# Two-layer graph network, one core: the one-hots' numbers and the directions are read from PSUM instead of SBUF

## What is computed

```python
# layer 0
h   = x @ W_lin.T
ef  = shifted_softplus(gaussian(edge_weight) @ Wf1 + bf1) @ Wf2 + bf2      # (edges, 128)
agg = segment_sum(h[src] * ef, dst)
x   = layernorm(x + shifted_softplus(agg @ Wm1 + bm1) @ Wm2 + bm2)
# layer 1: 32 scalars and 32 vectors of 3 per node
w  = silu(silu(emb(edge_weight) @ w0 + b0) @ w1 + b1) @ w2 + b2            # 4 x 32 per edge
Y1 = sqrt(3) * edge_attr / |edge_attr|                                      # directions (edges, 3)
ss, vv = (x[:, :32] @ W_up0)[src], (x[:, 32:] @ W_up1)[src]
m0, m3 = w[0] * ss, w[3] * (vv . Y1)
m1, m2 = w[1] * ss * Y1, w[2] * vv
x = layernorm(x + segment_sum([m0, m3, m1, m2], dst) @ W_out)
```

## Time and profile before

| | us |
|---|---|
| median of 3 runs (2197.67 to 2209.35) | 2200.56 |
| profiled execution, its own time | 2202.79 |
| span of the profiled execution | 2201.0 |
| busy: PE / DVE / ACT / POOL | 1899.1 / 1370.4 / 637.9 / 1569.6 |
| granted clock of PE, mean | 0.823 |

### The profile page before, as it was taken

How to read it: one execution, slowest core, us unless ns; L and a number is a source line. 1 busy time by engine, 2 the same in 40 slices (tenths; PEclk the granted TensorE clock), 3 DMA queues, 4 the chain that set the end, 5 groups by cost and what they waited for, 6 DMA issues and landing times.

```text
span 2201.0 us, 34359 instructions
## 1 busy us (share of the span) xinstructions
PE 1899.1 (86%) x10138; PEld 1431.4 (65%) x10138; DVE 1370.4 (62%) x2905; ACT 637.9 (29%) x995; POOL 1569.6 (71%) x1599
## 2 busy tenths in 40 slices
PE   5887877778777887777879999999999999899997
PEld 4665666666666666666557777666776676677766
DVE  6755555555555555555645776666667666666665
ACT  3643343343433433432541111111111111111114
POOL 4777777777777777777147777777777777777770
PEclk8777777777777777777867998898999998988889
DMA  7422222222222222222021111111121221111112
GB/s 217 126 78 78 76 81 76 76 81 76 76 81 76 80 76 76 81 76 62 6 82 51 55 54 53 53 54 54 53 55 54 54 55 54 52 55 54 53 52 66
DMA packets 105683, 152.31 MB, mean 69 GB/s; under 512 B 33982, under 2 KB 65490, under 8 KB 105546
## 3 DMA queue, kind: packets, MB, share of 16 engines
q0 software_dynamic: 50656, 103.11, 17.3%
q1 hardware_dynamic: 54652, 46.76, 7.0%
q10 hardware_dynamic: 336, 2.01, 0.3%
HBM read 138.53 MB, written 13.21 MB: 69 GB/s over the span
## 4 chain that ended last, share of the span: by engine, by line
POOL 68%; issue 22%; PE 7%; DMA 1%; DVE 1%; ACT 1%; SPq 0%; POOLq 0%; DVEq 0%; ACTq 0%
POOL sent L436 68%; DMA unit_in<-in_x 1%; PE bank L984 1%; PE bank L800 1%; PE bank L767 1%; PE bank L815 1%; PE bank L953 1%; PE bank L759 1%; PE bank L988 0%; PE bank L942 0%; PE bank L871 0%; PE bank L879 0%; PE bank L802 0%; DMA sent<-up_table,senders 0%; DMA sent<-h_table,senders 0%
## 5 line engine op out<-in xcount | busy, mean ns | idle before, releaser
L436 POOL DMA_INDIRECT sent<-up_table,senders x784 | 775.3, 989 | 268.2 <-issue 237.7
L436 POOL DMA_INDIRECT sent<-h_table,senders x784 | 766.5, 978 | 263.9 <-issue 238.6
L815 PE MATMUL bank<-onehot,msg 128*128 128x128 f32 x4704 | 794.0, 332 | 7.1 <-DVE sums L1098 4.2
L815 PEld LDWEIGHTS bank<-onehot,msg 128*128 128x128 f32 x4704 | 706.4, 235 | 116.0 <-issue 91.4
L800 PE MATMUL bank<-Wf_sb,hid 128*128 128x128 f32 x1568 | 281.1, 334 | 94.8 <-DVE hid L1114 94.5
L1124 DVE TENSOR_TENSOR msg<-bank,sent 128x512 f32<-128x512 f32 x196 | 135.6, 692 | 349.1 <-issue 189.7
L800 PEld LDWEIGHTS bank<-Wf_sb,hid 128*128 128x128 f32 x1568 | 246.0, 239 | 153.5 <-DVE hid L1114 100.2
L800 PEld LDWEIGHTS bank<-w_sb,h 64*128 64x128 f32 x1568 | 195.5, 193 | 213.1 <-issue 116.2
L631 ACT ACTIVATE soft<-soft 128x512 f32<-128x512 f32 (+1 forms) x209 | 131.2, 628 | 591.2 <-DVE soft L1105 558.4
L1085 DVE TENSOR_TENSOR onehot<-relT,iota 128x512 f32<-128x512 f32 x392 | 268.8, 686 | 39.3 <-PE bank L815 37.1
L800 PE MATMUL bank<-w_sb,h 64*128 64x128 f32 x1568 | 233.9, 291 | 47.3 <-DVE msg L1157 46.4
(11 more groups left out here) (133 smaller groups left out, 1330.4 us busy)
## 6 DMA issues: line engine op xcount, KB each, us to landing
basis<-in_edge_weight SPq DMA_DIRECT2D x196, 100.0 KB
sent<-h_table,senders POOLq DMA_INDIRECT x784
sent<-up_table,senders POOLq DMA_INDIRECT x784, 2.5
basis<-near_lengths SPq DMA_DIRECT2D x196, 16.0 KB
radial_embedding<-basis SPq DMA_DIRECT2D x196, 16.0 KB
emb_in<-radial_embedding SPq DMA_DIRECT2D x98, 32.0 KB
unit_in<-in_x SPq DMA_DIRECT2D x12, 256.0 KB, 3.7
h_table<-h SPq DMA_DIRECT2D x12, 256.0 KB, 2.8
```

The costliest lines, as they stand in the source:

```text
L436: pool.indirect_dma_start(sent[:, n % SLOTS, j, :], None, table, bass.IndirectOffsetOnAxis(pick, 0))\
L815: last = t_.matmul(ps[:, k, :], msg[:, p, j, k * P:(k + 1) * P], onehot[:, p, j, :], start=(j == 0), stop=(j == HALF_CHUNKS - 1))
```

## The change

Three operands of DVE move from SBUF to PSUM.

- ACT copies `iota` into columns 384 to 511 of banks 4 and 5 (`numbers`), once before each layer. `one_hots` reads `numbers[p]` of its half's parity. DVE waits for the copies once before each layer's loop (`s_numbers`).
- In layer 1, ACT copies the 12 direction numbers per partition of a half into bank 6 or 7 (`ways`), in its step h for half h-2, after the messages of half h-4 are made. Lines 1138 and 1153 read `ways`. DVE waits for `L1["ways"]` ahead of line 1138.
- The copy stands at the head of ACT's step, ahead of the silu of the same step. ACT's loop runs two steps longer.
- The directions are signalled by `s_dirs`; DVE's own wait behind them goes.

```diff
+    ways = [b[:, 0:3 * HALF_CHUNKS].rearrange("p (j c) -> p j c", c=3) for b in bank[6:8]]
+    numbers = [b[:, HALF - WINDOW:] for b in winps]
...
+        def number_windows():
+            for q in range(2):
+                a.activation(numbers[q], iota[:, :], ACT.Copy).then_inc(s_numbers, 1)
+        act.wait_ge(s_const, 9)
+        number_windows()
...
+        act.wait_ge(norm0["dve"], WIDE + last_unit + 1)
+        act.wait_ge(norm0["act"], WIDE + last_unit + 1)
+        number_windows()
+        act.wait_ge(s_dirs, 1)
+
+        def copy_ways(h):
+            b = h.before(2)
+            wait(act, L1["msg"], b.upto())
+            a.activation(ways[h.parity], dirT[:, :, :, :].rearrange("p a b c -> p (a b) c")
+                         [:, at(h.number(HALF_CHUNKS), HALF_CHUNKS), :], ACT.Copy)\
+                .then_inc(L1["ways"], 1)
 
         def layer1(h):
+            b = h.before(2)
+            if b.real():
+                copy_ways(b)
             if h.parity == 0 and h.real():
...
-        for_halves(act, iterations, layer1, 0)
+        for_halves(act, iterations, layer1, 2)
...
-                            iota[:, :].rearrange("p (a n) -> p a n", a=1)
+                            numbers[p].rearrange("p (a n) -> p a n", a=1)
...
-            dirs = dirT[:, :, :, :].rearrange("p a b c -> p (a b) c")
-            dirs = dirs[:, at(h.number(HALF_CHUNKS), HALF_CHUNKS), :]\
-                .rearrange("p j (c m) -> p j c m", m=1).broadcast_to(cube)
+            dirs = ways[p].rearrange("p j (c m) -> p j c m", m=1).broadcast_to(cube)
+            wait(dve, L1["ways"], h.upto())
```

More of the change, by code:

```diff
@@ L323, in build @@
     s_norm = sem("s_norm")
+    s_numbers = sem("s_numbers")
+    s_dirs = sem("s_dirs")
     def unit_sems(phase):
@@ L347, in edge_sems @@
         own = (("squared", "basis", "capped", "exped", "logged", "soft"),
-               ("act1", "filt2", "act2", "dots", "scaled", "dot"))[layer]
+               ("act1", "filt2", "act2", "dots", "scaled", "dot", "ways"))[layer]
         return by_dma | {k: sem(f"L{layer}_{k}") for k in
@@ L1273, in _ @@
         flag = dve.value_load(sorted_flag[0:1, 0:1], min_val=0, max_val=1)
+        dve.wait_ge(s_numbers, 2)
         with dve.If(flag):
@@ L1371, in _ @@
         then(v.reciprocal(norm, norm))
[L1372 to L1375, removed]
+        v.tensor_tensor(raw.rearrange("p (e c) -> p e c", c=3),
+                        raw.rearrange("p (e c) -> p e c", c=3),
+                        norm.rearrange("p (e a) -> p e a", a=1)
+                        .broadcast_to([P, all_chunks, 3]), ALU.mult).then_inc(s_dirs, 1)
         dve.wait_ge(s_zeroed, 1)
         flag = dve.value_load(sorted_flag[0:1, 0:1], min_val=0, max_val=1)
+        dve.wait_ge(s_numbers, 4)
         with dve.If(flag):
```

## The result

| | before | after |
|---|---|---|
| median of 4 runs, us | 2203.03 (2197.67 to 2209.35) | 2146.71 (2141.71 to 2148.30) |
| profiled execution / its span, us | 2202.79 / 2201.0 | 2146.51 / 2144.6 |
| busy PE / DVE / ACT / POOL, us | 1899.1 / 1370.4 / 637.9 / 1569.6 | 1828.1 / 1364.5 / 664.7 / 1508.9 |
| granted clock of PE, mean | 0.823 | 0.865 |

The ratio is 0.9739, 95% interval 0.9707 to 0.9772: 2.6% faster. The forecast was 2145. (The kernel before has one run more here than in its own table.)

What follows compares the result with a forecast made beforehand. The prediction took the number of gathers times their period as the bound in both layers: 2202.8 - 25.0 - 35.3 + 4 = 2146.5 for the profiled execution, which lay 2.2 above the median, so 2145; range 2138 to 2160, chance 0.75.

Steps and rivals of the forecast that it cites:

- Terms 1 and 2: Gathers of layers 0 and 1: time above the 944 ns floor goes, gaining 25.0 and 35.3 us.
- What counts is the second SBUF input, not the length or the opcode: DVE beside POOL's gathers: two SBUF inputs hold a gather starting meanwhile until 0.82 us after the operation's end.
- Term 3: DVE's operations with a PSUM input: between -8 and +60 ns each, taken as 0.
- Term 4: Two ACT copies of the numbers before each layer: cost 0, or 1.4 us a layer without cover.
- Term 5: ACT's queue in layer 1: the new wait makes PE stand some 1.1 us a pair; cost put at 4 us.
- the PE-bound rival: Layer 1: PE's clock stays at 0.83, POOL waits for messages, the layer 1 gain is lost; 2185, chance 0.12.
- The closed loop: Layer 1, messages through PE and DVE to messages two halves on: 9.0 us a pair, below the gathers' 9.98.
- the slower clock: Layer 1: PE's stand lets its clock fall to 0.76, 11.7 us a pair; 2304, chance 0.06.
- table loads: ACT in layer 1: copies and silus need different tables, four loads of 1.28 us a pair; 2300, chance 0.03.

Runs made afterwards that it cites:

- the dose: Changed kernel plus, per half of layer 0, one extra DVE comparison of 768 elements with two SBUF inputs; 2186.51 us (0.9907).
- e6: Changed kernel plus, per half of layer 0, an extra DVE scalar operation, a multiplication by 1.0 with one SBUF input; 2149.99 us (0.9735).
- e3: Changed kernel with ACT's copy of the directions moved behind the silu of the same step; 2148.89 us (0.9737).
- e1: Changed kernel with the directions read from SBUF again and ACT's copy of them gone, numbers left in PSUM; 2149.23 us (0.9748).
- e2: Changed kernel with one-hots compared with iota in SBUF again, directions left in PSUM; 2201.65 us (0.9973).
- b1: e3 with the squares of the directions made by ACT instead of DVE; 2141.25 us (0.9714).
- the cover taken away: Changed kernel with two of the four gathers of each half in layer 1 left out; layer 1's gathers took 948.0 us.

## Why the prediction was right

- Terms 1 and 2. Forecast 25.0 and 35.3 us, measured 25.1 and 35.7. The part that makes the gain was right in its mechanism and in its size. The hold was read rightly: a gather that starts under the operation ends 0.82 us after it. All 186 held gathers of the dose end 0.811 to 0.828 us after the operation (504.36 + 0.95 + 0.82 = 506.13 = 504.89 + 1.24 in the rows above), as those in the earlier trace rows do.
- "What counts is the second SBUF input, not the length or the opcode" was right for this change and too narrow as a rule (e6).
- Term 3. 0 taken; with a PSUM input DVE's lines became 7 to 9 ns shorter (one-hots 686 to 679, `dots` 558 to 551, line 1153 554 to 545). The 65 ns more that the Trainium skill's page "Perfetto Trace Analysis", section "Optimizing Scalar/DVE Operations", gives for the engine's busy time did not show: from the start of line 1153 to that of the next operation it was 0.468 us before and is 0.464 after (medians).
- Term 4. 0 taken, 0.4 and 0.5 us seen ahead of the layers. Over all profiles these two stretches vary from 43.6 to 46.1 us and from 83.7 to 86.3, so this is no cost that the runs can tell.
- Term 5. 4 us taken for PE's stand and put at the start of layer 1. The stand came (PE waits 50.2 us for ACT at line 907), but its cost did not show: layer 1 is 980.7 us with it and 980.6 without (e3), and POOL's wait for messages is 7.1 us in one profile of the changed kernel and 3.2 in another, for 4.4 before. What filled the place of the 4 us is 3.5 us behind the last gather, where the last 32 window and output matmuls ran at half clock. The prediction had no such term. e3, without the stand, has these two slow groups as well (3.80 and 3.76 us), so the stand does not make them. What does is open: the end takes 51.6 us before, 51.5 in e1 and 52.8 in e2, and 54.0 to 56.2 in seven of the eight profiles with all three operands in PSUM and all gathers, but 51.7 in b1. So the gain was understood, and that the sum gave 2146.5 for an execution of 2146.51 is luck.
- The range had two slips. Its low end by its own words is 2140 - 4 = 2136 and not 2138, and its high end of 2160 does not take in the PE-bound rival, which stands at 2185. Neither mattered here.
- The closed loop was forecast at 9.0 us a pair at full clock and 9.7 on the mean. With the cover taken away it is 9.7 on the mean. That the stand would be 1.1 us there too was wrong, as said above. The mean clock in 1180 to 2040 us rose from 0.90 to 0.94 with the stand; with the copy behind it was 0.89, with layer 1 as long. The two lines are of the changed kernel and of e3 (stretch, us, PE busy, clock, DMA share, GB/s). The rivals of the slower clock and of the PE-bound layer fall.

```profile
1180.00:2040.00 860.00, 816.23 (x4698) 0.94 0.21 56
1180.00:2040.00 860.00, 844.42 (x4687) 0.89 0.21 56
```

- No table loads came between the copies and the silus; ACT's copy takes 183 ns.

## What to carry to other kernels

When an engine that issues indirect DMAs is the bound, look at the spread of its instruction, not only its mean. Here a floor of 944 ns with a tail was a conflict, and the end of the long ones, nearly always 0.82 us behind another engine's operation, named the partner. One operand moved to another memory can remove it without touching the amount of work. A wait put at the head of an engine's queue delays what stands behind it; the room beside the bound (here 10.0 against 9.7 us a pair) says whether it is seen.

## What the runs showed of the hardware

- The hold has one direction for two-input operations. In the kernel before, 217 one-hots started in the first 0.7 us of a gather and took 0.68 to 0.70 us, where the median of all is 0.68; only those under way at its start hold it.
- For the scalar operation it has both. It lasts 548 ns at the least, 684 in the median, and the excess depends on the gather that it starts in:

```profile
L1235 DVE TENSOR_SCALAR dots<-relT x196: 548/684/794, 62.0 to 1032.6; 128x768 f32<-128x768 f32 x196
```

```profile
514.69 0.95 POOL L441 DMA_INDIRECT sent<-h_table,senders  x1 [0.30 <-issue]
515.28 0.74 DVE L1235 TENSOR_SCALAR dots<-relT 128x768 f32<-128x768 f32 x1
```

It ends at 516.02, which is 0.55 us after 515.47: it seems to have stood until 0.78 us after the gather's start. The same working gives 0.77 to 0.785 us in 177 of the 182 places where it starts in that part of a gather; the other five, all ahead of 101 us, ran at once, and in three of them the gather took 1057 to 1143 ns instead. That the first part of a gather reads and the rest writes would fit both directions, but no run here shows it.
- Two kernels that differ only in the copy's place had PE clocks of 0.94 and 0.89 in layer 1 and the same length of it: where PE has idle time beside the bound, its clock is no measure of the time.
